# Mean square from a Gram diagonal in the gate's products, with bias additions on GpSimd

## What is computed

```python
bias = braak_embed[braak_stages][..., None]
q = query + bias                                  # x plus one number per row and sequence
attn = softmax(einsum('bsd,btd->bst', q, key))    # key and value are the same tensor, side
o = einsum('bst,btd->bsd', attn, value)

nx = o * rsqrt(mean(o * o, axis=-1) + EPS) * norm_w
probs = softmax(nx @ gate_w.T); topw, topi = top_k(probs, 2)
# two experts (base weights plus low-rank parts) per row, weighted; out = x + ffn(nx)
```

## Time and profile before

| | |
|---|---|
| median of 3 runs | 1332.32 us (1332.14 to 1332.47) |
| profiled execution | 1332.48 us, span from first to last instruction 1330.3 us |
| busy share | PE 99%, PEld 87%, DVE 65%, ACT 41%, POOL 17% |
| granted TensorE clock, all 40 slices | 9 or more tenths |
| DMA | 69.57 MB, mean 52 GB/s; in 16.0 to 30.6 us a share of 0.96 at 288 GB/s |

### The profile page before, as it was taken

One profiled execution on the slowest core, in us unless ns is written; L12 is line 12 of the kernel. 1 busy time (PEld: TensorE's weight loads), 2 busy tenths in 40 slices (PEclk: granted clock), 3 DMA queues, 4 the chain that ended last, 5 costly groups with the idle time before them and its releaser, 6 DMA issues.

```text
span 1330.3 us, 18656 instructions
## 1 busy us (share of the span) xinstructions
PE 1317.7 (99%) x7396; PEld 1154.4 (87%) x7396; DVE 864.4 (65%) x1541; ACT 547.6 (41%) x1022; POOL 221.2 (17%) x170
## 2 busy tenths in 40 slices
PE   7999999999999999999999999999999999999998
PEld 7999998888888888888888888888888888888887
DVE  5787665765677566756675667657765767565655
ACT  5877773433343333333433324333433333333332
POOL 2333341020202020202020201102020202020200
PEclk9999999999999999999999999999999999999999
DMA  8344631020101101020202020202010110202000
GB/s 281 120 143 144 190 114 40 2 72 1 56 17 36 38 22 51 2 72 0 72 2 71 1 71 2 72 0 72 0 58 17 30 42 7 67 1 71 1 17 17
DMA packets 59359, 69.57 MB, mean 52 GB/s; under 512 B 7034, under 2 KB 46344, under 8 KB 59016
## 3 DMA queue, kind: packets, MB, share of 16 engines
q1 hardware_dynamic: 59248, 68.38, 16.7%
q10 hardware_dynamic: 24, 0.01, 0.0%
HBM read 51.27 MB, written 17.10 MB: 51 GB/s over the span
## 4 chain that ended last, share of the span: by engine, by line
PE 98%; DVE 1%; ACT 1%; DMA 0%; issue 0%; ACTq 0%; DVEq 0%
PE bank L1096 30%; PE bank L1097 30%; PE bank L1098 30%; PE bank L1142 2%; PE bank L1192 2%; PE bank L1170 1%; PE bank L1198 1%; PE bank L1135 1%; ACT prob L594 0%; ACT qT_hi L583 0%; DMA embed_in<-in_L_cond_braak_embed 0%; ACT kT_hi L584 0%; DVE act_br L983 0%; DVE act_b L980 0%; DVE br_lo L993 0%
## 5 line engine op out<-in xcount | busy, mean ns | idle before, releaser
L972 DVE TENSOR_TENSOR act_a<-silu_a,bank 128x512 f32<-128x512 f32 x128 | 87.6, 685 | 252.9 <-PE bank L1098 237.1
L673 ACT ACTIVATE br_hi<-act_br 128x512 fp32r<-128x512 f32 x128 | 81.0, 633 | 188.7 <-DVE act_br L983 188.7
L666 ACT ACTIVATE silu_b<-bank 128x512 f32<-128x512 f32 x128 | 76.2, 596 | 191.8 <-PE bank L1098 191.0
L662 ACT ACTIVATE silu_a<-bank 128x512 f32<-128x512 f32 x128 | 76.0, 594 | 175.6 <-PE bank L1098 175.5
L1098 PE MATMUL bank<-w2T_hi,s_lo 128*128 128x256 f32 x512 | 144.9, 283 | 0.0
L1097 PE MATMUL bank<-w2T_lo,s_hi 128*128 128x256 f32 x512 | 144.8, 283 | 0.0
L1096 PE MATMUL bank<-w2T_hi,s_hi 128*128 128x256 f32 x512 | 144.2, 282 | 0.0
L980 DVE TENSOR_TENSOR act_b<-silu_b,bank 128x512 f32<-128x512 f32 x128 | 87.9, 687 | 76.0 <-PE bank L1098 75.1
L527 POOL TENSOR_TENSOR t_lo<-t_scaled,t_hi 128x1024 fp32r<-128x1024 f32 x16 | 38.3, 2392 | 553.9 <-ACT t_hi L654 553.9
L543 POOL TENSOR_TENSOR v_lo<-v_full,v_hi 128x512 fp32r<-128x512 f32 x64 | 94.5, 1508 | 139.0 <-ACT v_hi L658 139.0
L993 DVE TENSOR_TENSOR br_lo<-act_br,br_hi 128x512 fp32r<-128x512 f32 x128 | 104.6, 817 | 5.8 <-ACT br_hi L673 3.3
(11 more groups left out here) (177 smaller groups left out, 3296.2 us busy)
## 6 DMA issues: line engine op xcount, KB each, us to landing
x_in<-in_x SPq DMA_DIRECT2D x32, 256.0 KB, 3.0
kv<-in_fside_BxSxS SPq DMA_DIRECT2D x32, 256.0 KB, 3.1
t_scratch<-oT SPq DMA_DIRECT2D x32, 256.0 KB, 2.0
t_in<-t_scratch SPq DMA_DIRECT2D x16, 512.0 KB
x_out<-in_x SPq DMA_DIRECT2D x16, 512.0 KB, 3.8
out<-x_out SPq DMA_DIRECT2D x30, 256.0 KB, 5.8
rho<-scale_scratch SPq DMA_DIRECT2D x16, 256.0 KB
rstd<-scale_scratch SPq DMA_DIRECT2D x16, 256.0 KB
```

The lines of the kernel that those rows point to most:

```text
L662: nc.scalar.activation(silu_a[j % 2][:, :], h1_bank[j % 2][:, :], ACT.Silu).then_inc(silu_a_ready, 1)
L666: nc.scalar.activation(silu_b[:, :], h1_bank[j % 2][:, :], ACT.Silu).then_inc(silu_b_ready, 1)
L673: nc.scalar.activation(br_hi[j % 2][:, :], act_br[j % 2][:, :], ACT.Copy).then_inc(br_hi_ready, 1)
L972: nc.vector.tensor_tensor(act_a[j % 2][:, :], silu_a[j % 2][:, :], h3_bank[j % 2][:, :], ALU.mult).then_inc(act_a_ready, 1)
```

## The change

Five edits, in the words of the diff:

1. The oT buffers get a stride of 160 elements per block of 128, and columns 128 to 135 of each block hold a copy of gateT, placed there once per buffer by POOL (place_gate). The gate's product takes oT as the stationary and the block with its eight gate columns, 136 in all, as the moving operand. Columns 0 to 127 of the result are the Gram matrix of the output rows, its diagonal the sum of squares. The separate product with ones, the squaring on ACT and sum_squares on POOL go.
2. keep_gate multiplies each 128x128 Gram block by the identity with an accumulated sum (two operations), in place of the small mean_sq operation.
3. EPS * r * r is made once per routing group in route_copy; the row sums of all sequences are kept.
4. The bias additions move from DVE to POOL, except those of sequences 0 and 1. For c from 2 on they stand ahead of value_low(c), in steps 0 and 1 behind it.
5. PE issues 13 transposes of the identity into o_bank once the identity is ready, and 8 more after the transposes of gate_in (keep_clock). PE waits for const_ready 2 first, then 4.

```diff
+        O_STRIDE = P + 32
+        GATE = slice(P, P + E)
-        oT = [sb(early, f"oT{k}", [P, DC * S]) for k in range(2)]
-        oT_sq = [sb(early, f"oT_sq{k}", [P, DC * S]) for k in range(2)]
-        sq_sum = [sb(early, f"sq_sum{k}", [P, S]) for k in range(2)]
+        oT = [sb(early, f"oT{k}", [P, DC, SC, O_STRIDE]) for k in range(2)]
+        gram_diag = sb(early, "gram_diag", [P, SC, P])
...
-        GATE_STRIDE = 16
+        GATE_STRIDE = P + E
...
-                sp.dma_start(t_scratch[bass.ds(P * c, P), :], oT[c % 2][:, :]
+                sp.dma_start(t_scratch[bass.ds(P * c, P), :].rearrange("p (n s) -> p n s", s=P).rearrange(
+                             "p (d h) s -> p d h s", d=DC), oT[c % 2][:, :, :, 0:P]
...
+            def add_bias(c):
+                pool.wait_ge(q_ready, c)
+                pool.wait_ge(qkT_ready, c - 1)
+                pool.wait_ge(seq_loaded[c % RING], 32 * (c // RING + 1))
+                for h in range(SC):
+                    last = nc.gpsimd.tensor_scalar(q[c % 2][:, h, :], x_in[c % RING][:, h, :],
+                                                   bias[:, h, c:c + 1], None, ALU.add)
+                last.then_inc(q_ready, 1)
+
+            def place_gate(k):
+                pool.wait_ge(gate_w_copied, 1)
+                for dc in range(DC):
+                    last = nc.gpsimd.tensor_copy(oT[k][:, dc, :, GATE],
+                                                 gateT[:, dc, :].unsqueeze(1).to_broadcast([P, SC, E]))
+                last.then_inc(gate_placed, 1)
+
             def step(c):
+                if 2 <= c < BATCH - 2:
+                    add_bias(c + 2)
                 value_low(c)
-                if c >= 1:
-                    sum_squares(c - 1)
+                if c < 2:
+                    add_bias(c + 2)
+                    place_gate(c)
...
-                nc.scalar.activation(oT[c % 2][:, :], o_bank[:, :], ACT.Copy).then_inc(oT_copied, 1)
-                nc.scalar.activation(oT_sq[c % 2][:, :], o_bank[:, :], ACT.Square).then_inc(oT_squared, 1)
+                nc.scalar.activation(oT[c % 2][:, :, :, 0:P].rearrange("p d h s -> p (d h) s"),
+                                     o_bank[:, :].rearrange("p (n s) -> p n s", s=P), ACT.Copy).then_inc(oT_copied, 1)
...
-                nc.vector.scalar_tensor_tensor(eps_r2[:, :], r[:, :], EPS, r[:, :], ALU.mult, ALU.mult
-                                               ).then_inc(eps_ready, 1)
-                dve.wait_ge(eps_ready, c + 1)
                 halves = gate_bank[:, 0:SC * GATE_STRIDE].rearrange("p (h n) -> p h n", h=SC)
-                nc.vector.scalar_tensor_tensor(mean_sq[:, cols], halves[:, :, E], 1.0 / D,
-                                               eps_r2[:, :], ALU.mult, ALU.add)
-                nc.vector.tensor_scalar(logits[:, cols, :], halves[:, :, 0:E], 1.0, None,
-                                        ALU.mult).then_inc(gate_read, 1)
+                for h in range(SC):
+                    nc.vector.scalar_tensor_tensor(gram_diag[:, h, :], halves[:, h, 0:P], 1.0 / D, ident[:, :],
+                                                   ALU.mult, ALU.mult, accum_out=mean_sq[:, SC * c + h:SC * c + h + 1])
+                nc.vector.tensor_scalar(logits[:, cols, :], halves[:, :, GATE], 1.0, None, ALU.mult
+                                        ).then_inc(gate_read, 1)
...
-                link(r, 2, nc.vector.tensor_scalar(g_z[:, :], mean_sq[:, cols], 1.0, None, ALU.mult))
+                nc.vector.scalar_tensor_tensor(g_eps[:, :], row_sum[:, cols], EPS, row_sum[:, cols], ALU.mult, ALU.mult
+                                               ).then_inc(eps_ready, 1)
+                dve.wait_ge(eps_ready, r + 1)
+                link(r, 2, nc.vector.tensor_tensor(g_z[:, :], mean_sq[:, cols], g_eps[:, :], ALU.add))
...
-            pe.wait_ge(const_ready, 5)
+            def keep_clock(n):
+                for _ in range(n):
+                    nc.tensor.transpose(o_bank[:, 0:P], ident[:, :], ident[:, :])
+
+            pe.wait_ge(const_ready, 2)
+            keep_clock(13)
+            pe.wait_ge(const_ready, 4)
...
                 for h in range(SC):
                     for dc in range(DC):
-                        nc.tensor.matmul(gate_bank[:, h * GATE_STRIDE:h * GATE_STRIDE + E],
-                                         oT[c % 2][:, dc * S + h * P:dc * S + (h + 1) * P],
-                                         gateT[:, dc, :], start=(dc == 0), stop=(dc == DC - 1))
-                pe.wait_ge(sq_summed, c + 1)
-                for h in range(SC):
-                    col = h * GATE_STRIDE + E
-                    last = nc.tensor.matmul(gate_bank[:, col:col + 1], sq_sum[c % 2][:, h * P:(h + 1) * P],
-                                            ones[:, :], start=True, stop=True)
+                        last = nc.tensor.matmul(gate_bank[:, h * GATE_STRIDE:(h + 1) * GATE_STRIDE],
+                                                oT[c % 2][:, dc, h, 0:P], oT[c % 2][:, dc, h, 0:GATE.stop],
+                                                start=(dc == 0), stop=(dc == DC - 1))
                 last.then_inc(gate_ready, 1)
...
             last.then_inc(gate_wT_ready, 1)
+            keep_clock(8)
             for c in range(ROWS_STEP):
```

More of the change, by code:

```diff
@@ L83, in adaln_moe_ffn @@
         b2T = split("b2T", [ER, D])
-        ones = sb(ctx, "ones", [P, 1])
         rank_key = sb(ctx, "rank_key", [P, E])
@@ L90, in adaln_moe_ffn @@
         mean_sq = sb(ctx, "mean_sq", [P, COLS])
-        row_sum = [sb(ctx, f"row_sum{k}", [P, SC]) for k in range(RING)]
-        eps_r2 = sb(ctx, "eps_r2", [P, SC])
+        row_sum = sb(ctx, "row_sum", [P, COLS])
+        g_eps = sb(ctx, "g_eps", [P, GCOLS])
         g_logits = sb(ctx, "g_logits", [P, GCOLS, E])
@@ L114, in adaln_moe_ffn @@
         rt = [sb(ctx, f"rt{k}", [P, KT]) for k in range(2)]
-        sb(ctx, "pad_t", [P, 328])
+        sb(ctx, "pad_t", [P, 304])
+        O_STRIDE = P + 32
+        GATE = slice(P, P + E)
         early = ExitStack()
@@ L212, in adaln_moe_ffn @@
         oT_copied = sem("oT_copied")
-        oT_squared = sem("oT_squared")
-        sq_summed = sem("sq_summed")
+        gate_placed = sem("gate_placed")
         gate_ready = sem("gate_ready")
@@ L500, in _ @@
                                     base=0, pattern=[[-1, P]], channel_multiplier=1).then_inc(const_ready, 1)
-            nc.gpsimd.memset(ones[:, :], 1.0).then_inc(const_ready, 1)
             nc.gpsimd.iota(rank_key[:, :], pattern=[[-1, E]], base=E, channel_multiplier=0,
@@ L553, in _ @@
             v_low(0, 1)
-            sum_squares(BATCH - 1)
             v_low(0, 2)
@@ L595, in exp @@
                                                 bias=neg_max[c % 2][:, h:h + 1],
-                                                accum_out=row_sum[c % RING][:, h:h + 1])
+                                                accum_out=row_sum[:, SC * c + h:SC * c + h + 1])
                 last.then_inc(prob_ready, 1)
@@ L743, in _ @@
             dve.wait_ge(stage_loaded, 16 * STAGE_LOADS)
-            dve.wait_ge(const_ready, 5)
+            dve.wait_ge(const_ready, 4)
             nc.vector.tensor_copy(itok_f[:, :], itok_in[:, :]).then_inc(stage_ready, 1)
@@ L760, in weight_low, with add_first_bias @@
                 last.then_inc(w_lo_ready, 1)
[L763 to L766, removed]
+            def add_first_bias(c):
+                dve.wait_ge(seq_loaded[c], 32)
                 for h in range(SC):
-                    last = nc.vector.tensor_scalar(q[c % 2][:, h, :], x_in[c % RING][:, h, :],
-                                                   bias[:, h, bass.ds(c, 1)], None, ALU.add)
+                    last = nc.vector.tensor_scalar(q[c][:, h, :], x_in[c][:, h, :], bias[:, h, c:c + 1], None, ALU.add)
                 last.then_inc(q_ready, 1)
@@ L791, in keep_gate @@
                 dve.wait_ge(gate_ready, c + 1)
-                r = row_sum[c % RING]
                 cols = bass.ds(SC * c, SC)
-                nc.vector.scalar_tensor_tensor(eps_r2[:, :], r[:, :], EPS, r[:, :], ALU.mult, ALU.mult
-                                               ).then_inc(eps_ready, 1)
-                dve.wait_ge(eps_ready, c + 1)
                 halves = gate_bank[:, 0:SC * GATE_STRIDE].rearrange("p (h n) -> p h n", h=SC)
-                nc.vector.scalar_tensor_tensor(mean_sq[:, cols], halves[:, :, E], 1.0 / D,
-                                               eps_r2[:, :], ALU.mult, ALU.add)
-                nc.vector.tensor_scalar(logits[:, cols, :], halves[:, :, 0:E], 1.0, None,
-                                        ALU.mult).then_inc(gate_read, 1)
+                for h in range(SC):
[3 more added lines that the diff above has]
+                                        ).then_inc(gate_read, 1)
             ROUTE_OPS = 30
@@ L942, in step @@
                     keep_gate(c - 2)
-                if c + 2 < BATCH:
-                    add_bias(c + 2)
                 if jobs_here and c == 0:
```

(6 more changed lines are left out.)

## The result

The changed kernel takes 1322.97 us (median of four runs, 1321.57 to 1323.66) against 1332.28 before: ratio 0.9929, 95% interval 0.9912 to 0.9946, 9.3 us less. The forecast was 1321.6 us. The profiled execution took 1322.53 us, its span 1320.7, 9.6 less than the span of the earlier trace rows.

The account below looks back on a forecast made before the run. It took PE as the bound, busy 1317.7 of 1330.3 us. Gates 9.3, load stage 1.2 and a wait 0.2 made 10.7 us off 1332.48; with the median 0.16 lower, 1321.6 us, range 1318.6 to 1326.6.

Parts of the forecast that it names:

- The gate's products: PE in each sequence's gate: products with 136 columns take 0.96 us instead of 1.26, saving 0.30 us a sequence.
- GpSimd: Bias additions moved to GpSimd: 0.35 us each, 0.70 a pair (0.54 to 1.48), sum of squares of 738 ns dropped.
- the 0.85 us: Steps 0 and 1: addition behind value_low on GpSimd makes q late by 0.65 and 0.2 us, together 0.85.
- The load stage: First 31 us: earlier clock rise 2.7 us, less 0.85, plus 0.3 for one gate; 2.1 us, capped to 1.2 won.
- The cap at sequence 4: Load of sequence 4's side rows lands just before 28.63 us, limiting the loading gain to 1.2 us, not 2.1.
- Both are hidden: Steps from 2 on: GpSimd's addition ahead of value_low, and value_low behind it, cost PE nothing; without cover 0.7 us a step.
- the softmax cover: Each step, PE's wait for softmax output: slack falls from 0.57 to 0.27 us, still enough.
- The 0.2 us near 190: A softmax wait of 0.46 us near 190 us: 0.2 us won through the dropped square on ScalarE.
- Rival A: Loading: identity transposes leave the clock low, load stage some 0.5 us later, 1323.3 us; chance 0.18.
- C: Gate on PE: wide f32 products take four cycles a column or don't hide weight loads, 1349 us; chance 0.08.
- B: Steps: softmax cover fails, half of the gates' saving lost, 4.7 us, so 1326.3 us; chance 0.11.
- D: Steps: the change does nothing because ScalarE's chain takes PE's place at once, 1332 us; chance 0.03.

Follow-up runs that it names:

- e5: Changed kernel with blocks of price-measuring instructions added on PE and on POOL, results unused: 1363.46 us in a single execution.
- a1: The changed kernel measured again, unaltered, on another chip than e8: 1322.37 us, ratio 0.9925.
- e2: The kernel before with only the 13 and 8 identity transposes added: 1331.35 us, ratio 0.9994.
- e4: Changed kernel without the identity transposes, bias additions as changed on GpSimd: 1323.83 us, ratio 0.9939.
- e1: Changed kernel without the identity transposes and with all bias additions back on VectorE: 1323.62 us, ratio 0.9938.
- e3: Changed kernel with all bias additions on VectorE, identity transposes kept: 1322.68 us, ratio 0.993.
- e7: Changed kernel with the GpSimd bias addition as one two-input operation with broadcast bias column: 1321.79 us, ratio 0.9923.
- e8: Changed kernel with bias additions of sequences 2 and 3 on VectorE too, the rest on GpSimd: 1319.5 us, ratio 0.9907.
- e9: Changed kernel with additions of sequences 2 and 3 on VectorE, the rest one two-input GpSimd operation each: 1320.58 us, ratio 0.9913.

## Why the prediction was right, and which of its terms were not

The direction, the size and the range hold: 10.7 us were forecast, 9.3 measured. That the sum came within 1.4 us was luck: two wrong terms, +3.2 us for the gates and about -4.6 for all the rest, went against each other. One of the signs by which the prediction called itself wrong also came: PE waited for the additions beyond step 3.

- **The gate's products: right mechanism, mis-sized.** "8 x 0.12 = 0.96 us. Saved 0.30" was too little. e5 has 0.116 us at 136 columns and 0.1125 at 8. I had set 0.12 for each new record against an interval of 1.26 us that is shorter than its twelve records: in the old gate the second record starts 0.03 us after the first, where all others are 0.112 apart. The new gate is shorter in the same way, as attention starts 0.03 us after its last record. So what goes is four records of 0.1125 us, less 8 x 0.0035: 0.42 us. By the steps, 0.40. Over 32 gates 3.2 us more than forecast.
- **GpSimd: wrong, and outside its bounds.** "I take 0.35, nearest to the one-input copy" measured 0.927 us, above the upper end of 0.74 that I had taken from a two-input row. The kind of operation, not the number of inputs, sets the price (e5). Steps 0 and 1 were the right place: the mechanism of the 0.85 us there was right, and it cost 3.25 us.
- **The load stage** was to win 1.2 us and is 0.6 behind at step 3. Of the 2.7 us for the clock 1.78 came in the profiled run, as the rise came between 9.6 and 9.9 us there, not at 5; a1 has it at 5 and 2.52 us. The cap at sequence 4 is real for e2, but it isn't the load alone: of the 1.88 us for the pair in the earlier trace rows, three times the usual 0.61, some 1.3 us lie beside POOL's operations, the lock again. The prediction took that price as given and put the whole cap down to the load. In the changed kernel GpSimd's own delay in steps 1 and 2 was the larger.
- **"Both are hidden"** failed in part: additions ahead of value_low wait for a load (16.8 us of POOL's idle time), and in steps 25 and 28 q came too late for PE, which with step 18 makes 1.3 us. The late steps differ from profile to profile: a1 has 28, e4 has 29. I had named the queue and the waiter, but at a price of 0.70. That the load comes late there because the first tile's loads share the DMA queue is argued from its place, not shown.
- **ScalarE, the softmax cover and the Gram diagonal** were right: 0.27 us of cover held in the plain steps, and a Gram block costs 0.28 us with 0.08 for the accumulator. The 0.2 us near 190 didn't show: that step shrank by 0.44 us, like any other.
- **What moving the additions saves** I had not seen at all: on VectorE the second addition is locked out by value_low, and once the step is shorter PE waits for that q, 0.11 us a step (e1, e3).
- Rival A falls: its 1323.3 us is nearer to the measured time than my number, but the first scores came 0.12 us apart, with the clock up. C falls by e5. Of B a small part is true (late waits of 1.3 us against its 4.7), though mostly for GpSimd's additions and not for softmax. D falls.

## What to carry to other kernels

Price an operation on another engine by a row of the same kind of operation, not of the same size; GpSimd's tensor_scalar cost more than its two-input form here, with a scalar per partition and with an immediate. When a wait at the start and a gain in every step come with one edit, split it: the first two sequences want the fast engine, the others the quiet one, and that alone is worth 2.4 to 2.9 us here. And where PE is full, count records: up to 136 columns an f32 record cost next to nothing more (0.1125 us at 8 columns, 0.116 at 136).

## What the runs showed of the hardware

**The clock rose behind identity transposes, but not at a fixed time.** In a1, the same kernel as the changed one, the spacing falls within the bias product, behind 13 transposes and about two records of that product. Timeline of PE in a1:

```profile
1.51 3.04 PE L1114 MATMUL bank<-ident 128*128 128x128 f32 x13 [1.51 <-POOL ident L499]
4.48 0.80 PE L1122 MATMUL bank<-stage_hot,embed_in 6*128 6x32 f32 x4
5.20 0.66 PE L1154 MATMUL bank<-ident,kv 128*128 128x128 f32 x4
...
7.05 1.09 PE L1114 MATMUL bank<-ident 128*128 128x128 f32 x8
```

The same four transposes in the changed kernel's profile:

```profile
5.47 1.11 PE L1154 MATMUL bank<-ident,kv 128*128 128x128 f32 x4
```

There the spacing falls only between 9.6 and 9.9 us, and the five others with these fillers (e2, e3, e7, e8, e9) have it between 9.6 and 11.0 us, against 13.7 without fillers. So 2.52 or 1.78 us are won in step 0, by chance of the execution. The spread of 2 us between executions fits that, but which of the others rose early isn't on record. The Trainium skill's page "TensorE: Matmul & The Clock Gate", Part 4, has it that the full clock doesn't engage for transposes. The rows of a1 speak against it, and the measurement decides; but it is one profile of seven, and the last records before its rise are products.

**The clock fell with PE never idle.** Stretches of PE in e5 (busy us of each engine, PEclk is the granted clock):

```profile
124.84:126.19 1.35, 1.35 (x15) 1.35 (x14) 1.09 (x4) 0.12 (x2) 1.35 (x3) 1.00 0.60 177
126.19:129.88 3.69, 3.69 (x22) 3.69 (x22) 0.00 (x0) 0.00 (x0) 0.69 (x1) 0.59 0.49 150
129.88:133.97 4.09, 4.09 (x21) 4.09 (x22) 0.00 (x0) 0.00 (x0) 0.00 (x0) 0.54 0.00 0
133.97:136.22 2.25, 2.25 (x22) 2.25 (x21) 0.00 (x0) 0.00 (x0) 0.00 (x0) 1.00 0.00 0
```

Behind the records of 8 columns, in those of 64, the level went from 2.4 to 1.2 GHz (a mean of 0.59 and 0.54 of full speed), and it was back for the records of 128. PE was busy for all of it. By single records the spacing is 0.21 us instead of 0.11 from 126.9 to about 133.7 us. That is why the records of 64 and 112 columns average 0.18 and 0.20 us. What makes it fall was not tested further.

**The store in four runs of 512 bytes per partition** issues in 0.525 us (median of 32), where one run of 2 KB took 0.339, and lands 2.5 us after issue, not 2.0. No instruction is shown waiting for it.
